# Narrow attentions of a one-core Trainium2 kernel: values and sums of two slices in one 32-column tile, six passes a batch for ten, merged by masked copies and a shuffle

## Chip, core and metric

The kernel runs on one core of one Trainium2 chip. The metric is the device time of one execution in microseconds (us), the median of the runs shown.

## What is computed

Four layers act on a residual `x` of 4 batches x 512 rows x 128 features. Each layer adds a cross-attention to 154 context rows and then a mixture of experts, each scaled by the tanh of a gate. Three of the four cross-attentions (layers 0, 2 and 3; the profile's names begin with L0x, L2x, L3x) have 16 heads of 8 features, and one function of the kernel makes all three:

```python
x = x + tanh(g_xattn[i]) * attention_i(layernorm(x), ctx)   # i = 0, 2, 3: 16 heads of 8
# attention: softmax(q k^T * scale) v, heads side by side, then @ Wo (+ bias)
x = x + tanh(g_ffn[i]) * experts_i(layernorm(x))
```

The softmax of a head needs two sums over the 154 keys: of weight times value (8 features) and of the weights alone. The kernel makes both on TensorE and divides afterwards.

## The kernel before, in words

`narrow_attention` (L800) writes out five instruction streams by hand (SyncE, GpSimd, TensorE, ScalarE, VectorE) that meet in counted semaphores. It loops over the 4 batches `b`; while the products of batch `b` are made, the scores of batch `f = b + 1` are made for their row maxima, and rows and queries of `g = b + 2` are prepared.

The 16 heads are 4 lanes (`j`, 32 partitions each) x 4 groups (`c`). The 154 keys are cut into 128 and a tail of 26, and the tails of all four groups share a fifth slice. So a batch has five slices (`SLOTS = 5`): c = 0..3 are the first 128 keys of one group, slice 4 (`NG`) is the tails.

On TensorE each batch goes through 12 score units `scores(f, i, i+1)` (L1134 to L1151), S0 to S11 here. All of them, for batches 1 to 3, write banks 0 and 1; so each waits until VectorE has taken the maxima of the one before (`maxima`, L1602, the reduction at L1611: `pe.wait_ge(s["mx"], n)`). Units have 3, 3 and 2 column blocks in turn: S2, S5, S8 and S11 are short. Between the units the stream places other work: `scoresT(b, c)` (L1161) makes the scores transposed, ScalarE's `exps` (L1398) makes weights of them in `pT` (two slices deep); `products(b, c)` (L1182, matmul L1198) multiplies by the values into bank 6 (`OUT`), and `sums(b, c)` (L1201, matmul L1210) multiplies the same weights by ones into bank 7 (`SUMS`). Each is a pass of four matmuls with 32 columns, one in each lane:

```python
nc.tensor.matmul(psum[32*j:32*j+32, OUT, :],  vz[:, b, x:x+32], pT[...], start=(c == 0), stop=(c == NG))   # products
nc.tensor.matmul(psum[32*j:32*j+32, SUMS, :], core.oz[:, c, :], pT[...], start=(c == 0), stop=(c == NG))   # sums
```

That is 5 + 5 passes a batch. `vz` holds each head's 8 value columns among zeros, in blocks 136 wide, so that the window of group c has its values in columns 8c to 8c + 7; `oz` has ones there. The order on TensorE within a batch is S0, row maxima, sums of the last tails, S1, scoresT 1, products 0, S2, queries, sums 0, S3, scoresT 2, S4, products 1, S5, sums 1, scoresT 3, S6, products 2, output of batch b - 1, S7, row maxima, sums 2, S8, scoresT 4, S9, products 3, S10, sums 3, S11, scoresT 0 and products of the tails (L1271 to L1330). The last batch (b = 3) has no score units; there `output(b-1, 1)` stands between the sums of slice 0 and scoresT 2.

After the tails ScalarE's `values` (L1406) copies both banks to SBUF (`ov`, `rsum`). VectorE's `normalised` (L1615) takes the reciprocal of 128 columns and multiplies, four times a batch, placed between the maxima of the next batch (after units 1, 2, 4 and 5); in the last batch it takes all 512 columns at once (L1746, L1759). TensorE's `output` (L1214) then multiplies each 128 columns by Wo as soon as they are there, `added` (L1628) adds the residual, `kept_in_parts` or `keep_rows` makes the next norm's statistics.

Ahead of the loop VectorE's `contexts` (L1541) fills `vz` and `vt` (values of the tails). `setup` (L82) makes constants on GpSimd; VectorE ends it with two copies (L181, L182).

Of the kernel before, what the change touches and what calls it, by code (L numbers as in the profile page):

```python
# [44 lines left out]
class Core:  # L45


    def __init__(self, nc, ctx):
# [33 lines left out]
def setup(core, io, loads, first):  # L82
# [3 lines left out]
    with ExitStack() as scope:  # L86
# [9 lines left out]
        with nc.Block() as block:  # L96
# [11 lines left out]
            def _(pool):  # L108
# [17 lines left out]
                nc.gpsimd.memset(core.oz[:], 0.0).then_inc(groups, 1)  # L126
# [5 lines left out]
                for c in range(4):  # L132
                    nc.gpsimd.memset(core.oz[:, c, 8 * c:8 * c + 8], 1.0)
# [5 lines left out]
                pool.wait_ge(groups, 7)  # L139
# [29 lines left out]
            def _(dve):  # L169
# [630 lines left out]
def narrow_attention(core, L, w, gate, kind, loaded, n_loads, late_loads=(), router=None, dispatch=None, pending=None):  # L800
# [21 lines left out]
    with ExitStack() as scope:  # L822
# [10 lines left out]
        vt = sb("vt", [P, B, NG, NG, DK])  # L833
# [4 lines left out]
        rsum = sb("rsum", [P, SEQ])  # L838
# [81 lines left out]
        with nc.Block() as block:  # L920
# [122 lines left out]
            def _(pe):  # L1043
# [138 lines left out]
                def products(b, c):  # L1182
                    n = SLOTS * b + c
                    if n < 0:
                        return
                    pe.wait_ge(s["pt"], NG * (n + 1))
                    if c == 0:
                        pe.wait_ge(s["vz"], b + 1)
                        pe.wait_ge(s["vt"], b + 1)
                        if b:  # L1190
                            pe.wait_ge(s["ov"], 2 * b - 1)
                        elif rope:
# [69 lines left out]
                if rope:  # L1262
                    pe.wait_ge(s["mx"], UNITS - 2)
                    keysT(1, SUMS)
                    queriesT(1, OUT)
                    pe.wait_ge(s["mx"], UNITS)
                if not rope:
                    pe.wait_ge(s["mx"], UNITS)
                    pe.wait_ge(s["bvb"], 1)
                    nc.tensor.matmul(psum[:, OUT, 0:D], bvb[:], w["wo"][:], start=True, stop=True).then_inc(s["bias_ps"], 1)  # L1270
                for b in range(B):  # L1271
# [24 lines left out]
                    sums(b, 0)  # L1296
# [12 lines left out]
                    sums(b, 1)  # L1309
# [8 lines left out]
                    sums(b, 2)  # L1318
# [10 lines left out]
                    sums(b, 3)  # L1329
# [12 lines left out]
            def _(act):  # L1342
# [2557 lines left out]
```

## Time and profile before

| | us |
|---|---|
| median of 3 runs | 1576.43 |
| lowest, highest run | 1574.64, 1577.44 |
| profiled execution, span from first to last instruction | 1592.2 |
| TensorE busy in it | 1297.0 |
| VectorE busy in it | 946.5 |
| ScalarE busy in it | 723.1 |

No time of the profiled execution beside its span is given; it was taken with the profiler on, and its span is 15.8 us (1.0%) above the median of the runs. Busy shares are averages over stages with different limits. In a row of the timeline the first two numbers are start and duration in us, and the bracket at the end gives the idle time of the engine before it and what ended that. An instruction that follows on the same engine can start a little before the duration of the one ahead is over.

### The profile page before, as it was taken

The numbers are of one execution on the slowest core, as the hardware profiler recorded it, in microseconds if no ns is written. First come the engines' busy times: TensorE is split into PE (matmuls) and PEld (weight loads), VectorE is DVE, ScalarE is ACT, GpSimd is POOL, SyncE is SP. The second block draws the span as 40 slices with busy tenths as digits, with TensorE's granted clock in tenths as the row PEclk, the third lists the DMA queues.
The fourth block names the chain that finished last, engine by engine and source line by source line (L and its number), as shares of the span: only waits on it lengthen the run. The fifth ranks groups of instructions, "written<-read, shape, count | busy, mean of one in ns | idle before, by whom it ended". The sixth has DMA issues, their size and how long they took to land. (4 is left out here: it accounts for less than half of the span.)

```text
span 1592.2 us, 25277 instructions
## 1 busy us (share of the span) xinstructions
PE 1297.0 (81%) x8946; PEld 752.5 (47%) x8946; DVE 946.5 (59%) x2139; ACT 723.1 (45%) x1940; POOL 527.5 (33%) x625
## 2 busy tenths in 40 slices
PE   2799629579989977784997698989887977996998
PEld 2444317345656645463442455656554434442443
DVE  6466621444555655255664688888764875555664
ACT  3354413166656533342543465655755333454222
POOL 2320340525333361333100365656643320000444
PEclk8599859799999997895998799999988996998999
DMA  2444120330000002322000000000000001000000
GB/s 65 127 130 128 40 66 26 72 75 14 1 1 2 1 27 62 89 58 50 9 10 2 1 1 1 1 2 1 1 1 1 1 10 23 10 3 1 7 7 14
DMA packets 66991, 45.30 MB, mean 28 GB/s; under 512 B 17564, under 2 KB 60261, under 8 KB 66869
## 3 DMA queue, kind: packets, MB, share of 16 engines
q1 hardware_dynamic: 61013, 34.48, 8.4%
q0 software_dynamic: 4096, 8.40, 1.9%
q8 instruction: 74, 1.21, 0.3%
q10 hardware_dynamic: 1760, 0.82, 0.3%
q14 instruction: 48, 0.39, 0.1%
HBM read 24.91 MB, written 13.89 MB: 24 GB/s over the span
## 5 line engine op out<-in xcount | busy, mean ns | idle before, releaser
L3411 ACT ACTIVATE L2a_pr<-psum,L2a_negmax 128x512 f32<-128x512 f32 (+3 forms) x256 | 132.6, 532 | 94.0 <-DVE L2a_negmax L3537 40.1
L557 ACT ACTIVATE L1x_praw<-psum,L1x_negmax 128x154 f32<-128x154 f32 x256 | 96.5, 392 | 78.4 <-DVE L1x_negmax L649 78.2
L318 POOL TENSOR_TENSOR L1x_pm<-L1x_praw,L1x_total 128x1024 f32<-128x1024 f32 x32 | 60.7, 1898 | 160.6 <-DVE L1x_total L655 111.7
L3276 PE MATMUL psum<-ident,L2a_pr 128*128 128x128 f32 x640 | 85.9, 278 | 19.0 <-DVE L2a_pT L3550 11.7
L649 DVE TENSOR_REDUCE L1x_negmax<-psum 128x4 f32<-128x616 f32 x64 | 50.7, 794 | 55.2 <-PE psum L370 51.0
L3276 PEld LDWEIGHTS psum<-ident,L2a_pr 128*128 128x128 f32 x640 | 71.7, 143 | 24.7 <-issue 21.1
L1978 POOL TENSOR_TENSOR L3f_scaled<-L3f_sg,L3f_wide 128x512 f32<-128x512 f32 (+1 forms) x44 | 55.7, 1271 | 66.9 <-ACT L3f_sg L2057 37.9
L1611 DVE TENSOR_REDUCE L3x_negmax<-psum 128x6 f32<-128x924 f32 (+1 forms) x48 | 47.7, 1011 | 46.8 <-PE psum L1149 37.4
L1611 DVE TENSOR_REDUCE L0x_negmax<-psum 128x6 f32<-128x924 f32 (+1 forms) x48 | 47.8, 1010 | 44.9 <-PE psum L1149 40.6
L3161 POOL TENSOR_TENSOR L2a_pr<-L2a_pr,L2a_total 128x1024 f32<-128x1024 f32 x29 | 56.5, 1947 | 46.5 <-DVE L2a_total L3566 46.3
L3164 POOL TENSOR_TENSOR L2a_pr<-L2a_pr,L2a_total 128x768 f32<-128x768 f32 x32 | 48.7, 1520 | 70.0 <-DVE L2a_total L3566 69.7
L1611 DVE TENSOR_REDUCE L2x_negmax<-psum 128x6 f32<-128x924 f32 (+1 forms) x48 | 47.8, 1011 | 32.6 <-PE psum L1149 27.8
L1404 ACT ACTIVATE L3x_pT<-psum 128x512 f32<-128x512 f32 x80 | 41.4, 606 | 50.3 <-PE psum L1175 41.8
L1404 ACT ACTIVATE L2x_pT<-psum 128x512 f32<-128x512 f32 x80 | 41.4, 605 | 49.0 <-PE psum L1175 40.5
L2057 ACT ACTIVATE L3f_sg<-psum 128x512 f32<-128x512 f32 (+1 forms) x44 | 26.3, 598 | 66.8 <-PE psum L2000 66.8
L3556 DVE COPY L2a_pT<-psum 128x768 f32<-128x768 f32 (+1 forms) x64 | 54.2, 846 | 3.3 <-PE psum L3276 3.3
L370 PE MATMUL psum<-L1x_kT,L1x_qT 64*128 64x154 f32 x512 | 52.6, 327 | 3.9 <-ACT L1x_qT L538 3.0
L1404 ACT ACTIVATE L0x_pT<-psum 128x512 f32<-128x512 f32 x80 | 41.4, 605 | 30.2 <-PE psum L1175 23.6
L3411 ACT ACTIVATION_READ_ACCUMULATOR L2a_pr<-psum,L2a_negmax 128x1 f32 x256 | 53.5, 209 | 0.0
L557 ACT ACTIVATION_READ_ACCUMULATOR L1x_praw<-psum,L1x_negmax 128x1 f32 x256 | 52.9, 207 | 0.0
L2878 PE MATMUL psum<-L1f_gu,L1f_xsT 128*128 x92 | 51.2, 645 | 1.1 <-ACT L1f_xsT L2931 1.1
L2000 PE MATMUL psum<-L3f_xnT,expert_arena 128*128 128x512 f32 (+1 forms) x88 | 46.7, 614 | 4.2 <-PEq L3822 4.2
(741 smaller groups left out, 3372.1 us busy)
## 6 DMA issues: line engine op xcount, KB each, us to landing
expert_arena<-in_L_ffn_w SPq DMA_DIRECT2D x16, 256.0 KB, 4.4
group_in<-zero SPq DMA_DIRECT2D x2, 1472.0 KB, 9.3
L1f_xs<-group_in SPq DMA_DIRECT2D x10, 256.0 KB, 3.8
group_out<-L1f_ys SPq DMA_DIRECT2D x10, 256.0 KB, 3.6
L1f_gu<-in_L_ffn_gate_up_w SPq DMA_DIRECT2D x8, 256.0 KB, 3.5
slots_in<-zero SPq DMA_DIRECT2D x1, 1280.0 KB, 9.0
L0f_xs<-slots_in SPq DMA_DIRECT2D x5, 256.0 KB, 3.6
resid<-in_x SPq DMA_DIRECT2D x4, 256.0 KB, 5.8
```

The lines of the kernel that those rows point to most:

```text
L318: nc.gpsimd.tensor_tensor(pm[:, n % 2].rearrange("p j t k -> p (j t) k"), praw[:, n % 3, :, :, 0:MAIN].rearrange("p j t k -> p (j t) k"), ...
L370: last = nc.tensor.matmul(psum[:, 2 * u + j, x * CTX:(x + 1) * CTX], qT[rows, g, t * P:(t + 1) * P], kT[rows, g, :], start=True, stop=True)
L557: nc.scalar.activation(praw[:, n % 3, j, t, :], psum[:, 2 * u + j, x * CTX:(x + 1) * CTX], ACT.Exp, bias=negmax[:, n % 2, u, j, x:x + 1], ...
L649: nc.vector.tensor_reduce(negmax[:, n % 2, u].rearrange("p j x -> p (j x)").rearrange("p (j x) -> p j x", x=2), psum[:, 2 * u:2 * u + 2, 0 ...
L1404: nc.scalar.activation(pT[:, (n % 2) * NG + j, :], psum[:, LANES + j, :], ACT.Exp, scale=scale).then_inc(s["pt"], 1)
L1611: nc.vector.tensor_reduce(negmax[:, f % 2, half, 2 * h:2 * h + 2, off:off + count], psum[:, bank:bank + 2, 0:count * CTX].rearrange("p j ( ...
L1978: nc.gpsimd.tensor_tensor(scaled[0:rows, n % 2, :], sg[0:rows, n % 3, :], wide[0:rows, picked_to(n) % SLANT, :], ALU.mult).then_inc(s["sca ...
L2878: nc.tensor.matmul(psum[:, UP[i % len(UP)], :], xsT[:, q % 2, t * P:(t + 1) * P], w["gu"][:, bass.ds(expert[i], 1), :].rearrange("p a f -> ...
L3161: ins = nc.gpsimd.tensor_tensor(x, x, inv[:, 0:2].unsqueeze(2).to_broadcast([P, 2, SEQ]), ALU.mult)
L3276: last = nc.tensor.transpose(psum[:, TURN + n // 4, n % 4 * P:(n % 4 + 1) * P], pr[:, m % RING, n * P:(n + 1) * P], core.ident[:])
L3411: ins = nc.scalar.activation(pr[:, i % RING, SEQ * j + lo:SEQ * j + hi], psum[:, bank + j, lo:hi], ACT.Exp, bias=negmax[:, i % RING, e:e + ...
L3556: nc.vector.tensor_copy(pT[:, q % 2, t:t + 7:3, heads, :], src[:, :, 0:3 * P].rearrange("p j (k x) -> p k j x", x=P))
```

## The change

The window of a group gets its ones beside its values: for groups 0 and 1 values go to rows 0 to 15 of a lane and sums to rows 16 to 31 of one bank (`EARLY`), for groups 2 and 3 sums go to rows 0 to 15 and values to rows 16 to 31 of the other (`LATE`). Four product passes and two tail passes make both. ScalarE splits the early bank by a mask per partition (`core.half`, columns 4 and 5) into `sm` and `ov`; VectorE adds the other half of the late bank to each, then swaps the halves of `sm` with a stream shuffle, so that sums stand on the rows of their values. The calls on VectorE move by one or two units.

```diff
-    LANES, OUT, SUMS = 2, 6, 7
+    LANES, EARLY, LATE = 2, 6, 7
+    SWAP = [(x + 16) % 32 for x in range(32)]
...
# TensorE: products and sums of five slices become products of four and two tails
-    nc.tensor.matmul(psum[32 * j:32 * j + 32, SUMS, :], core.oz[:, c, :] if c < NG else core.ot[:]..., ...)
+    pe.wait_ge(s["split"], 2 * b)       # before products 0, b > 0
+    pe.wait_ge(s["merged"], 2 * b)      # before products 2, b > 0
+    last = nc.tensor.matmul(psum[32 * j:32 * j + 32, EARLY if c < 2 else LATE, :], vz[:, b, x:x + 32], ..., start=(c % 2 == 0), stop=False)
+  def tail(b, late_half):
+    last = nc.tensor.matmul(psum[32 * j:32 * j + 32, LATE if late_half else EARLY, :], vt[b][:, j, 32 * late_half:32 * late_half + 32], ..., start=False, stop=True)
+    last.then_inc(s["pv" if late_half else "early"], 1)
...
-    products(b - 1, NG)
+    tail(b - 1, 0)
     scores(f, 0, 1)
     max_rows(2 * b + 1, lane(b, 0, 0))
-    sums(b - 1, NG)
+    tail(b - 1, 1)
...
-    sums(b, 0)
...
-    sums(b, 1)
...
-    sums(b, 2)
...
-    sums(b, 3)
...
# ScalarE
-    nc.scalar.activation(ov[:], psum[:, OUT, :], ACT.Copy).then_inc(s["ov"], 1)
-    nc.scalar.activation(rsum[:], psum[:, SUMS, :], ACT.Copy).then_inc(s["ov"], 1)
+    act.wait_ge(s["early"], b + 1)
+    nc.scalar.activation(sm[:], psum[:, EARLY, :], ACT.Identity, scale=core.half[:, 5:6]).then_inc(s["split"], 1)
+    nc.scalar.activation(ov[:], psum[:, EARLY, :], ACT.Identity, scale=core.half[:, 4:5]).then_inc(s["split"], 1)
...
+  def ones_in():     # five activations that write ones into vz and vt; called once, after filled(2)
...
# VectorE
-    nc.vector.tensor_tensor(vt[:, f], ...)
+    for half in range(2):
+        ins = nc.vector.tensor_tensor(vt[f][:, :, 48 * half:48 * half + 16]..., ...)
...
+  def merged(b, what):
+    if what == 0:
+        dve.wait_ge(s["pv"], SLOTS * (b + 1))
+    if what < 2:
+        dve.wait_ge(s["split"], 2 * b + 1 + what)
+        to, side = ((sm, 4), (ov, 5))[what]
+        nc.vector.scalar_tensor_tensor(out=to[:], in0=psum[:, LATE, :], scalar=core.half[:, side:side + 1], in1=to[:],
+                                       op0=ALU.mult, op1=ALU.add).then_inc(s["merged"], 1)
+    else:
+        dve.wait_ge(s["merged"], 2 * b + 1)
+        nc.vector.stream_shuffle(oT[:], sm[:], SWAP).then_inc(s["swapped"], 1)
...
     maxima(f, 1, 2)
-    normalised(b - 1, 0, 1)
+    merged(b - 1, 0)
     maxima(f, 2, 3)
-    normalised(b - 1, 1, 2)
+    merged(b - 1, 2)
     query_squares(g)
     maxima(f, 3, 4)
+    merged(b - 1, 1)
+    normalised(b - 1, 0, 1)
     maxima(f, 4, 5)
     query_inverted(g)
+    normalised(b - 1, 1, 2)
+    maxima(f, 5, 6)
     normalised(b - 1, 2, 3)
-    maxima(f, 5, 6)
+    maxima(f, 6, 7)
     normalised(b - 1, 3, 4)
-    maxima(f, 6, 7)
+    maxima(f, 7, 8)
     added(b - 1)
...
# last batch
+    for what in (0, 2, 1):
+        merged(b - 1, what)
     normalised(b - 1, 0, QT)
...
-    normalised(B - 1, 0, QT)
+    for what in (0, 2, 1):
+        merged(B - 1, what)
+    for t in range(QT):
+        normalised(B - 1, t, t + 1)
...
# setup: oz and its four memsets go; a mask `half` is made on GpSimd, and at the end of VectorE's stream
+    dve.wait_ge(groups, 9)
+    nc.vector.tensor_reduce(core.half[:, 4:5], core.half[:, 0:4], X_AXIS, ALU.add).then_inc(parts_made, 1)
+    dve.wait_ge(parts_made, NT + 2)
+    nc.vector.tensor_scalar(core.half[:, 5:6], core.half[:, 4:5], -1.0, 1.0, ALU.mult, ALU.add)
```

## Rows read from the trace of the kernel before

**Rows 1.** The page, parts 1 and 2: engines, and TensorE's granted clock in tenths.

```profile
PE 1297.0 (81%) x8946; PEld 752.5 (47%) x8946; DVE 946.5 (59%) x2139; ACT 723.1 (45%) x1940; POOL 527.5 (33%) x625
...
PEclk8599859799999997895998799999988996998999
```

**Rows 2.** Groups by line, layer 2's attention: count, busy us, mean ns, idle before.

```profile
L1210 PE MATMUL psum<-L2x_pT,oz 128*32 128x512 f32 x128 | 17.0, 604 | 0.0
```

**Rows 3.** Timeline of TensorE, layer 2, batch 1, units S2 to S7.

```profile
792.30 0.79 PE L1149 MATMUL psum<-L2x_k,L2x_q 32*128 32x154 f32 x8
...
794.08 1.07 PE L1210 MATMUL psum<-L2x_pT,oz 128*32 128x512 f32 x8
795.08 0.66 PE L1149 MATMUL psum<-L2x_k,L2x_q 32*128 32x154 f32 x6
...
797.35 1.05 PE L1149 MATMUL psum<-L2x_k,L2x_q 32*128 32x154 f32 x12 [0.36 <-DVE L2x_negmax L1611]
...
799.63 0.79 PE L1149 MATMUL psum<-L2x_k,L2x_q 32*128 32x154 f32 x8 [0.23 <-DVE L2x_negmax L1611]
...
802.31 0.95 PE L1149 MATMUL psum<-L2x_k,L2x_q 32*128 32x154 f32 x12
...
805.27 1.05 PE L1149 MATMUL psum<-L2x_k,L2x_q 32*128 32x154 f32 x12
...
806.79 1.06 PE L1210 MATMUL psum<-L2x_pT,oz 128*32 128x512 f32 x8
```

**Rows 4.** Timeline of VectorE in the same stretch.

```profile
798.45 1.12 DVE L1611 TENSOR_REDUCE L2x_negmax<-psum 128x6 f32<-128x924 f32 x1 [1.16 <-PE psum L1149]
799.49 0.94 DVE L1622 RECIPROCAL L2x_rsum<-L2x_rsum 128x128 f32<-128x128 f32 x1
800.47 0.29 DVE L1626 TENSOR_TENSOR L2x_oT<-L2x_ov,L2x_rsum 128x128 f32<-128x128 f32 x1
800.68 0.79 DVE L1611 TENSOR_REDUCE L2x_negmax<-psum 128x4 f32<-128x616 f32 x1
```

**Rows 5.** Groups by line, layer 2's attention: operations of VectorE and ScalarE on 128x512.

```profile
L1365 ACT ACTIVATE L2x_qc<-psum,L2x_bqc 128x512 f32<-128x512 f32 x2 | 1.4, 690 | 1.4 <-PE psum L1090 1.4
...
L770 DVE TENSOR_SCALAR resid<-L2x_oT 128x512 f32<-128x512 f32 x2 | 0.9, 427 | 0.1
...
L1509 DVE TENSOR_TENSOR L1f_gu<-L1f_dn 128x512 f32<-128x512 f32 x1 | 0.7, 679 | 0.0
```

**Rows 6.** Timeline of layer 2's last batch: VectorE and TensorE.

```profile
848.33 3.35 DVE L1622 RECIPROCAL L2x_rsum<-L2x_rsum 128x512 f32<-128x512 f32 x1 [3.72 <-ACT L2x_rsum L1413]
...
867.70 3.35 DVE L1622 RECIPROCAL L2x_rsum<-L2x_rsum 128x512 f32<-128x512 f32 x1 [11.76 <-ACT L2x_rsum L1413]
...
873.61 0.75 DVE L1634 SCALAR_TENSOR_TENSOR L2x_oT<-psum,gate,resid 128x512 f32<-128x512 f32 x1 [1.63 <-PE psum L1225]
...
852.16 1.13 PE L1225 MATMUL psum<-L2x_wo,L2x_oT 128*128 128x128 f32 x8 [2.09 <-DVE L2x_oT L1626]
```

**Rows 7.** Timeline of layer 3's last batch, TensorE: output of batch 2.

```profile
1437.87 1.13 PE L1225 MATMUL psum<-L3x_wo,L3x_oT 128*128 128x128 f32 x8 [2.25 <-DVE L3f_lg L1875]
```

**Rows 8.** Timeline at the end of layer 0's attention: GpSimd and VectorE.

```profile
191.07 0.96 POOL L2376 DMA_INDIRECT slots_in<-L0f_pair,L0f_to  x1 [0.30 <-issue]
191.31 0.17 DVE L774 TENSOR_SCALAR stat<-L0x_mv 128x8 f32<-128x8 f32 x1
```

**Rows 9.** Timeline ahead of the loops: VectorE in setup, ScalarE in layer 2.

```profile
12.49 0.47 DVE L182 TENSOR_SCALAR ctxp<-ctxT 128x616 f32<-128x616 f32 x1
...
747.85 0.59 ACT L1396 ACTIVATE L2x_mrow<-psum 8x512 f32<-8x512 f32 x1 [6.50 <-PE psum L1158]
```

**Rows 10.** Stretches: us, busy us (and count) of each engine, then the granted clock.

```profile
853.50:856.90 3.40, 3.40 (x20) 0.60 (x20) 2.33 (x11) 1.75 (x4) 0.00 (x0) 0.50 0.02 5
...
850.10:853.50 3.40, 1.34 (x12) 1.25 (x16) 2.66 (x6) 0.26 (x1) 0.00 (x0) 1.00 0.00 0
...
1433.80:1437.20 3.40, 1.82 (x16) 0.31 (x15) 3.37 (x4) 1.47 (x4) 0.00 (x0) 1.00 0.00 0
```

More of the change, by code:

```diff
@@ L125, in _ @@
                 nc.gpsimd.memset(core.quad[:], 1.0).then_inc(groups, 1)
-                nc.gpsimd.memset(core.oz[:], 0.0).then_inc(groups, 1)
+                nc.gpsimd.memset(core.half[:], 1.0).then_inc(groups, 1)
                 nc.gpsimd.memset(core.pen64[:], 0.0).then_inc(groups, 1)
@@ L138, in _ @@
                                         pattern=[[32, 4]], channel_multiplier=-1).then_inc(groups, 1)
-                pool.wait_ge(groups, 7)
+                nc.gpsimd.affine_select(out=core.half[:, 0:4], in_=core.half[:, 0:4], compare_op=ALU.is_ge, fill=0.0, base=0,
+                                        pattern=[[-32, 4]], channel_multiplier=1).then_inc(groups, 1)
+                pool.wait_ge(groups, 8)
+                nc.gpsimd.affine_select(out=core.half[:, 0:4], in_=core.half[:, 0:4], compare_op=ALU.is_ge, fill=0.0, base=15,
+                                        pattern=[[32, 4]], channel_multiplier=-1).then_inc(groups, 1)
                 nc.gpsimd.tensor_copy(core.ot[:], core.quad[:].unsqueeze(2).to_broadcast([P, 4, 8]))
@@ L832, in narrow_attention @@
         vz = sb("vz", [P, B, NG * WIDE])
-        vt = sb("vt", [P, B, NG, NG, DK])
+        vt_own = sb("vt", [P, B - 1, NG, 64])
+        vt = [vt_own[:, b] for b in range(B - 1)] + [core.x1[:, 14:16, :].rearrange("p n d -> p (n d)").rearrange("p (j e) -> p j e", j=NG)]
         negmax = sb("negmax", [P, 2, 2, NG, 2 * QT])
@@ L1180, in scoresT, with early_free @@
                                 last.then_inc(s["s2"], 1)
[L1182 to L1192, printed above, removed]
+                def early_free(b):
+                    pe.wait_ge(s["vz"], b + 1)
+                    pe.wait_ge(s["vt"], b + 1)
+                    if b:
+                        pe.wait_ge(s["split"], 2 * b)
+                    else:
+                        pe.wait_ge(s["ones_in"], 5)
+                        if rope:
                             pe.wait_ge(s["qc"], 2)
@@ L1333, in _ @@
                     dispatch.rowsT(pe, 1, 2, dispatch.rows, 1)
-                products(B - 1, NG)
-                sums(B - 1, NG)
+                tail(B - 1, 0)
+                tail(B - 1, 1)
                 if dispatch:
@@ L1450, in _ @@
                 filled(2)
+                ones_in()
                 if pending:
@@ L1561, in contexts @@
                     nc.vector.tensor_copy(heads[:, :, :, 0:DK], bank[:, 256:384].rearrange("p (c j d) -> p c j d", c=NG, j=NG)).then_inc(s["vz"], 1)
-                    nc.vector.tensor_tensor(vt[:, f], bank[:, 384:512].rearrange("p (c j d) -> p j c d", c=NG, j=NG),
-                                            core.quad[:].unsqueeze(1).unsqueeze(3).to_broadcast([P, NG, NG, DK]), ALU.mult).then_inc(s["vt"], 1)
+                    tails = bank[:, 384:512].rearrange("p (c j d) -> p j c d", c=NG, j=NG)
+                    for half in range(2):
+                        own = slice(2 * half, 2 * half + 2)
+                        ins = nc.vector.tensor_tensor(vt[f][:, :, 48 * half:48 * half + 16].rearrange("p j (c d) -> p j c d", c=2), tails[:, :, own, :],
+                                                      core.quad[:, own].unsqueeze(1).unsqueeze(3).to_broadcast([P, NG, 2, DK]), ALU.mult)
+                    ins.then_inc(s["vt"], 1)
                 def squares(x, rows, root):
```

90 lines of the change are left out of this document (54 added, 36 removed).

## The prediction, made before any run of the changed kernel

> **What bounds the kernel now.** I read the page first: TensorE is busy 81% of the span, VectorE 59%, ScalarE 45%, and the granted clock stands near full in the slices of the three narrow attentions (about 55 to 190, 755 to 875 and 1335 to 1460 us) [rows 1]. That says only that TensorE is the engine to watch. Then the groups by line of layer 2's attention: the sums have 128 records there, with 32 more for the tails, at 604 ns each [rows 2]. These overlap, so the price of a pass is read from the timeline: sums 0 starts at 794.08 and the next work at 795.08, 1.00 us [rows 3].
>
> Last the timelines of TensorE and VectorE side by side, unit by unit. Scores and maxima share one pair of banks, so units alternate. S4 starts at 797.35, its maxima at 798.45 take 1.12, S5 starts at 799.63 [rows 3, 4]: 2.28 us is the least for a long unit, however little stands in its gap. A short unit by the same steps: 0.79 scores, 0.05, 0.80 maxima, 0.06, so 1.70. TensorE's own scores take about 0.98 and 0.72 of this; a gap holds 1.30 or 0.98 of other work for nothing. Where it holds less, TensorE waits (0.36 and 0.23 before S4 and S5 [rows 3]). **So a removed pass is worth 1.00 only where its gap is overfull.**
>
> **What is removed.** Four passes a batch, 16 a layer, 48 in all: 48 us of TensorE at most. By gap:
> - Behind S2 (792.30 to 795.08, 2.78): queries and sums 0. Without the sums 1.78: 1.00 saved in batches 0 and 1. Batch 2 has no queries there, 0.72 + 1.00 = 1.72 against the least of 1.70: nothing.
> - Behind S5 (799.63 to 802.31, 2.68): sums 1 and scoresT 3. Without, 1.72: 0.96 saved in batch 0. In batches 1 and 2 a reciprocal and a multiplication stand ahead of the short maxima, which start 0.26 after the scores end instead of 0.05 [rows 3, 4]: 0.76.
> - Behind S7 (805.27 to 807.79, the latter being 806.79 + 1.00): row maxima and sums 2, 2.52. Without, the least of 2.28: 0.24. In layer 0, batches 0 and 1, a transposition of queries fills it further: 0.8.
> - Behind S10: sums 3 alone, 1.00 inside 1.30: nothing.
>
> **What is added and moved on VectorE.** The merge is a scalar_tensor_tensor of 128x512 from PSUM; L1634 is the same form, 0.75 [rows 6], 0.78 with its wait. Nothing in the trace is a shuffle. Its bounds are 0.43 (tensor_scalar, 128x512 in SBUF) and 3.35 (reciprocal, the slowest 128x512) [rows 5, 6]; I take 0.70, next to the tensor_tensor of that size, 0.68 [rows 5], which also moves one element in and out at a time. The Trainium skill (VectorE: DVE Perf Modes, The perf-mode tier table) gives a stream shuffle of 2,048 elements about 2.4 us, in the slowest tier; an estimate from it is 0.6 for 512, and the sum by it would be the same to within 1 us. No run here shows it yet.
>
> The first merge and the shuffle take the places of a reciprocal with its multiplication and are shorter: nothing. Two other places cost.
> - Between maxima 3 and 4 stand the second merge and the first reciprocal and multiplication. A reciprocal starts 1.04 after a reduction's start, the multiplication 0.98 after that, the next reduction 0.21 later [rows 4]: 1.04 + 0.78 + 0.98 + 0.21 = 3.01 from one long reduction to the next, where 2.28 is the least. S5 waits: 0.73 lost.
> - The fourth multiplication moves behind maxima 6, and the output of batch b - 1 behind S6 waits for it. S6 takes 0.95, 0.05 to its maxima, 1.04 + 0.98 + 0.29 to the product, about 0.3 for the last piece of output: 3.6 instead of 2.96 (802.31 to 805.27 [rows 3]). S7 and everything queued behind the output wait: 0.70 lost.
>
> Both hit batches 1 and 2. Products 2 now wait for both merges, with S7 and the output queued behind them on TensorE; the second merge follows maxima 3 and is over by then. Products 0 wait for both masked copies instead of one plain copy; these run in the same slots of ScalarE and end about as products 0 are due. `added`, a unit later, still ends as scoresT 4 needs its lane. Nothing for these three, and no DMA is moved: SyncE's queue keeps its order.
>
> **Sum of the loops.** Batch 0: 1.00 + 0.96 + 0.24 = 2.2 in layer 3; 1.85 in layer 2, where the pending rows of layer 1 fill VectorE behind maxima 2; 1.8 in layer 0, where squares of queries hold S4 and the first term falls away. Batch 1: 1.00 + 0.76 + 0.24 - 0.73 - 0.70 = 0.57 in layers 2 and 3, about 0 in layer 0. Batch 2: the same without the 1.00, a loss of 0.4, three times. Together 5.85 + 1.1 - 1.2 = **5.7 us saved**.
>
> **The last batch of each layer** has no score units. There the values of batch 2 are on the path: reciprocal at 848.33, output at 852.16 after 2.09 us of idle TensorE, then scoresT 2 [rows 6]; in layer 3 2.25 idle [rows 7]. Merge, shuffle, merge (0.78 + 0.72 + 0.78 = 2.3) replace two copies that ScalarE makes 0.5 apart; the masked copies themselves (Identity, 0.69 by L1365 [rows 5]) run under them. In layer 2 I get 849.6 instead of 848.33, 1.3 later; in the others 1.8. The sums that go shorten the way from scoresT 2 to the last slice again, by 1.3, 0.8 and 0.5 in layers 2, 3 and 0, since ScalarE's exponentials soon bind: 0, 1.0 and 1.3 late. TensorE then idles over 4 us, so some work there will run at half clock, as 853.5 to 856.9 does [rows 10]: 0.3, 0.5, 1.0. Behind the last tail: 1.0 for the merges, 0.4 for four reciprocals (4 x 1.18 against 3.35 + 0.9), less 0.7, as the output now runs under them: 0.7 each. Layer 0 ends with GpSimd at 192.03, VectorE at 191.48 [rows 8], so 0.5 of its delay is free. Ends: 2.5 + 1.0 + 2.2 = **5.7 us lost**.
>
> **Ahead of the loops.** Setup ends with VectorE's L182 [rows 9]; two small operations (0.17 each by L774 [rows 8]) and a wait follow it: 0.4. The second half of the tails' values delays layer 0's keys by 0.2. The five activations of ones are hidden in 6.50 us of idle ScalarE ahead of the row maxima [rows 9]; without that cover they would cost up to 5 x 0.69 a layer. GpSimd's setup loses and gains small operations: nothing.
>
> **Total:** 5.7 - 5.7 - 0.6, 0.6 us slower. The profiled span would be 1592.8 for 1592.2. The span stands 1.0% above the median of the runs; I carry the difference over: 1577.0.
>
> **Rivals.**
> - *VectorE hides its pieces.* If neither the 0.73 nor the 0.70 shows, six batches give 8.6 back: 1568.4. For it: VectorE is idle 1.16 ahead of a reduction [rows 4] and 41% of the span. Against it: both stand in its fixed order ahead of what TensorE waits for.
> - *TensorE's clock falls inside the loops*, slower. The loop now runs at 2.4 GHz; taken thinner, each of nine batches could lose one stretch as 853.5 to 856.9 to 1.2 GHz, 1.7 us each, 15 us: 1592. It decides from two such stretches in all (3.4 us). For it: the clock fell behind 2.09 idle us. Against: TensorE was busy 1.82 of 3.40 us around layer 3's 2.25 idle us and kept it, and the longest idle in a thinned loop is 1.3 [rows 7, 10]. The Trainium skill (TensorE: Matmul & The Clock Gate, Why this matters for your kernels) warns that idle gaps between bursts of matmuls put the engine back to half clock; by it, fewer passes can make the others dearer. The drop in rows 10 agrees, the kept clock shows that not every gap does it.
> - *The shuffle is dear.* At its upper bound 3.35 it adds 2.65 at six ends and, beyond 0.5 of slack, 2.2 in six batches: 29 us, 1606. It decides from about 1.1 us a shuffle. Only the range of unlike operations speaks for it.
>
> **Chances and range.** Forecast 0.55, its own range 1572 to 1582; hidden pieces 0.2; clock 0.1; shuffle 0.07; others, such as a wait I have overlooked, 0.08. A measurement of this kernel can tell about 0.2%, 3.2 us. The forecast case is mostly within it (0.45 of 0.55), with 0.06 above and 0.04 below; hidden pieces are faster but for 0.02; the clock and the shuffle slower but for 0.01; the rest is divided. Faster 0.24, same 0.49, slower 0.27. 1567 to 1586 leaves out most of the clock, the dear shuffle and the best of the hidden pieces.
>
> **What would show it.** Right: S2, S5 and S7 gaps of layer 2's batch 1 at 1.78, about 1.9 and 2.28; reduction 4 starting 0.7 late; TensorE waiting on the fourth multiplication ahead of S7; output of batch 2 in the last batch over 1 us later, and half clock behind it. Wrong: a loop batch shorter by 2 us or more, a shuffle far from 0.7 us, a granted clock of 0.5 between S0 and S11, or `ones_in` delaying the first row maxima.

## The result, and the profile after

The changed kernel takes 1610.62 us (median of 4 runs, 1603.22 to 1613.04) against 1576.93 for the kernel before beside it: a ratio of 1.021, 95% interval 1.019 to 1.023. It is 33.7 us slower; 1577.0 was forecast, with 1586 as the upper end. The profiled execution took 1608.59, its span is 1606.7. The mean granted clock of TensorE was 0.874 to 0.883 of full speed in the four runs, and 0.898 to 0.906 in ten runs of the kernel before (e6 below).

The page of the changed kernel, parts 1 and 2:

```profile
PE 1297.7 (81%) x8562; PEld 765.7 (48%) x8562; DVE 973.4 (61%) x2210; ACT 727.2 (45%) x1955; POOL 528.9 (33%) x623
...
PEclk8587758889999997896987799999998987897999
```

TensorE has 384 instructions fewer than in [rows 1] and is busy just as long: what it does takes longer. The clock line points at why. The third to fifth slice (80 to 200 us, most of layer 0's attention) stood at 9, 9, 8 and now stand at 8, 7, 7.

The first profile of before stood 16 us above its own runs, so the stages are compared with a second one, taken for e6 below (span 1572.4; the median of its runs is 1576.63). Stretches of batches 1 and 2 in layers 0, 2 and 3, each from the last row maxima of one batch to those of the next; columns are length, busy us (count) of TensorE, weight loads, VectorE, ScalarE and GpSimd, the granted clock, the share of the DMA engines and GB/s. The changed kernel:

```profile
95.36:135.33 39.97, 36.18 (x276) 20.86 (x274) 24.25 (x39) 17.13 (x31) 5.01 (x5) 0.69 0.46 118
135.33:170.44 35.11, 30.25 (x260) 15.34 (x256) 20.97 (x38) 14.13 (x26) 0.00 (x0) 0.79 0.39 101
782.55:812.72 30.17, 26.06 (x268) 13.55 (x270) 20.78 (x35) 13.93 (x27) 0.00 (x0) 1.00 0.07 12
812.72:846.40 33.68, 28.75 (x258) 15.24 (x256) 20.79 (x36) 12.32 (x24) 0.00 (x0) 0.81 0.01 2
1377.30:1409.19 31.89, 27.78 (x269) 13.66 (x270) 20.78 (x35) 14.26 (x27) 0.00 (x0) 0.96 0.06 11
1409.19:1438.47 29.28, 24.19 (x262) 12.67 (x264) 20.97 (x38) 14.14 (x27) 0.00 (x0) 1.00 0.01 2
sum 200.10, PE 173.20 PEld 91.33 DVE 128.54 ACT 85.91 POOL 5.01; mean PE 28.87 PEld 15.22 DVE 21.42 ACT 14.32 POOL 0.84
```

The kernel before (second profile), the same six stretches:

```profile
96.17:128.95 32.78, 30.61 (x312) 15.42 (x314) 22.42 (x36) 17.28 (x32) 5.05 (x5) 1.00 0.47 124
128.95:157.66 28.71, 27.67 (x294) 13.33 (x296) 19.16 (x34) 14.10 (x27) 0.00 (x0) 1.00 0.52 142
765.78:796.26 30.48, 29.37 (x300) 14.10 (x302) 19.00 (x32) 13.75 (x27) 0.00 (x0) 1.00 0.07 12
796.26:825.03 28.77, 27.66 (x294) 13.32 (x296) 18.99 (x31) 12.58 (x25) 0.00 (x0) 1.00 0.01 3
...
1379.44:1408.15 28.71, 27.66 (x294) 13.32 (x296) 19.16 (x34) 14.09 (x27) 0.00 (x0) 1.00 0.01 3
sum 179.93, PE 172.35 PEld 83.61 DVE 117.72 ACT 85.55 POOL 5.05; mean PE 28.72 PEld 13.93 DVE 19.62 ACT 14.26 POOL 0.84
```

Before, all six ran at 1.00. Now four of six have a lower clock, and the six together are 20.2 us longer. The two that kept 1.00 are near where the prediction put them: 30.17 for 30.48 (0.31 less; 0.57 was predicted) and 29.28 for 28.71 (0.57 more; 0.4 was predicted). Together these two are 0.3 us longer than before; the four at a lower clock carry 19.9 of the 20.2. The whole difference of the two spans, 34.3 us, by stages of the same two profiles:

| stage | before | after | difference |
|---|---|---|---|
| batches 1 and 2 of layers 0, 2, 3 | 179.9 | 200.1 | +20.2 |
| last row maxima to last transposed scores, three layers | 56.2 | 65.2 | +9.1 |
| from there to the end of the last output, three layers | 33.9 | 36.1 | +2.1 |
| first scores and batch 0, three layers | 155.2 | 152.3 | -2.9 |
| layer 2's last output to layer 3's first scores | 443.8 | 449.6 | +5.8 |
| all else | 703.4 | 703.3 | -0.1 |

**Where the clock falls.** TensorE in layer 2, from the output's wait in S6 to S9 or beyond, first batch 1, then batch 2, then a stretch of batch 2 with its granted clock (they answer to [rows 3]):

```profile
801.94 0.49 PE L1246 MATMUL psum<-L2x_wo,L2x_oT 128*128 128x128 f32 x2 [0.62 <-DVE L2x_oT L1678]
...
804.64 0.79 PE L1157 MATMUL psum<-L2x_k,L2x_q 32*128 32x154 f32 x8 [0.69 <-DVE L2x_negmax L1647]
...
806.46 1.05 PE L1157 MATMUL psum<-L2x_k,L2x_q 32*128 32x154 f32 x12
...
831.29 0.49 PE L1246 MATMUL psum<-L2x_wo,L2x_oT 128*128 128x128 f32 x2 [0.61 <-DVE L2x_oT L1678]
831.71 1.05 PE L1157 MATMUL psum<-L2x_k,L2x_q 32*128 32x154 f32 x12
...
833.98 1.40 PE L1157 MATMUL psum<-L2x_k,L2x_q 32*128 32x154 f32 x8 [0.69 <-DVE L2x_negmax L1647]
...
837.25 1.91 PE L1157 MATMUL psum<-L2x_k,L2x_q 32*128 32x154 f32 x12
...
844.16 0.63 PE L1157 MATMUL psum<-L2x_k,L2x_q 32*128 32x154 f32 x2 [1.29 <-DVE L2x_negmax L1647]
...
833.81:850.88 17.07, 15.61 (x108) 6.84 (x108) 6.19 (x16) 5.01 (x11) 0.00 (x0) 0.50 0.00 1
```

From S3 to the start of S8 the two batches are alike to 0.01 us: the output waits 0.6 for the fourth multiply, S8 waits 0.69 for the row maxima. Behind that, S9's scores take 1.91 instead of 1.05 in batch 2, where the granted clock is 0.5 (1.2 GHz) from 833.81 to 850.88, and batch 1 goes on at full clock. The longest idle time in either is 1.29 us; in batch 2 it comes only after the fall. In the kernel before S7 starts 2.96 behind S6; here it is 3.95, and S8 follows at 2.28.

Batch 1 has the work for its queries ahead of S3, which batch 2 has not. But batch 2 of layer 3 is like batch 2 of layer 2 to 0.01 us in every unit from S0 to S7, and it kept its clock:

```profile
1430.45 0.79 PE L1157 MATMUL psum<-L3x_k,L3x_q 32*128 32x154 f32 x8 [0.69 <-DVE L3x_negmax L1647]
...
1432.28 1.05 PE L1157 MATMUL psum<-L3x_k,L3x_q 32*128 32x154 f32 x12
```

The longest fall comes elsewhere. In layer 0's batch 1 the clock falls from 110.18 to 137.49, beginning in S4, ahead of the output's wait, behind an idle time of 1.65 us and within one of 0.83:

```profile
108.03 1.05 PE L1157 MATMUL psum<-L0x_k,L0x_q 32*128 32x154 f32 x12 [1.65 <-DVE L0x_negmax L1647]
...
110.91 0.62 PE L1157 MATMUL psum<-L0x_k,L0x_q 32*128 32x154 f32 x2 [0.83 <-DVE L0x_negmax L1647]
```

VectorE between the maxima of units 3 and 4 of batch 2, and ahead of the output (as [rows 4]):

```profile
821.81 1.12 DVE L1647 TENSOR_REDUCE L2x_negmax<-psum 128x6 f32<-128x924 f32 x1 [0.51 <-PE psum L1157]
822.85 0.74 DVE L1660 SCALAR_TENSOR_TENSOR L2x_ov<-psum,half,L2x_ov 128x512 f32<-128x512 f32 x1
823.50 0.94 DVE L1673 RECIPROCAL L2x_oT<-L2x_oT 128x128 f32<-128x128 f32 x1
824.48 0.29 DVE L1678 TENSOR_TENSOR L2x_oT<-L2x_ov,L2x_oT 128x128 f32<-128x128 f32 x1
824.69 1.11 DVE L1647 TENSOR_REDUCE L2x_negmax<-psum 128x6 f32<-128x924 f32 x1
...
830.94 0.29 DVE L1678 TENSOR_TENSOR L2x_oT<-L2x_ov,L2x_oT 128x128 f32<-128x128 f32 x1
```

One reduction follows the other by 2.88 (3.01 was predicted). The prices of the new operations, lines of the changed kernel by form (durations are least, median and greatest, in ns):

```profile
L1666 DVE STREAM_SHUFFLE L2x_oT<-L2x_sm x4: 716/721/731, 791.1 to 871.8; 128x512 f32<-128x512 f32 x4
...
L1660 DVE SCALAR_TENSOR_TENSOR L2x_ov<-psum,half,L2x_ov x4: 732/740/743, 793.5 to 872.4; 128x512 f32<-128x512 f32 x4
...
L1429 ACT ACTIVATE L2x_sm<-psum,half x4: 662/672/687, 787.2 to 870.1; 128x512 f32<-128x512 f32 x4
```

### The profile page after: what moved, and what is told of

It is laid out like the page before. It is cut to its first block and busy times, and to the rows that moved or that the text cites. A ratio compares the mean times of both kernels' runs of the same rounds, so it can differ in the third digit from the quotient of the medians.

```text
span 1606.7 us, 24645 instructions
## 1 busy us (share of the span) xinstructions
PE 1297.7 (81%) x8562; PEld 765.7 (48%) x8562; DVE 973.4 (61%) x2210; ACT 727.2 (45%) x1955; POOL 528.9 (33%) x623
## 5 line engine op out<-in xcount | busy, mean ns | idle before, releaser
L3471 ACT ACTIVATE L2a_pr<-psum,L2a_negmax 128x512 f32<-128x512 f32 (+3 forms) x256 | 132.0, 530 | 95.9 <-DVE L2a_negmax L3597 41.4
L563 ACT ACTIVATE L1x_praw<-psum,L1x_negmax 128x154 f32<-128x154 f32 x256 | 95.9, 390 | 79.2 <-DVE L1x_negmax L655 79.0
L3336 PE MATMUL psum<-ident,L2a_pr 128*128 128x128 f32 x640 | 85.7, 278 | 21.5 <-DVE L2a_pT L3610 12.9
L3336 PEld LDWEIGHTS psum<-ident,L2a_pr 128*128 128x128 f32 x640 | 71.7, 142 | 27.0 <-issue 23.3
L1647 DVE TENSOR_REDUCE L2x_negmax<-psum 128x6 f32<-128x924 f32 (+1 forms) x48 | 47.8, 1010 | 33.9 <-PE psum L1157 31.7
L1157 PE MATMUL psum<-L0x_k,L0x_q 32*128 32x154 f32 x384 | 45.5, 378 | 17.4 <-DVE L0x_negmax L1647 11.6
L1157 PEld LDWEIGHTS psum<-L0x_k,L0x_q 32*128 32x128 f32 x384 | 35.1, 237 | 46.2 <-DVE L0x_negmax L1647 30.2
```

Of the source, the lines that this page charges most:

```text
L563: nc.scalar.activation(praw[:, n % 3, j, t, :], psum[:, 2 * u + j, x * CTX:(x + 1) * CTX], ACT.Exp, bias=negmax[:, n % 2, u, j, x:x + 1], ...
L1157: last = nc.tensor.matmul(psum[:, bank + j % 2, k * CTX:(k + 1) * CTX], q4[rows, f % QB, c, t * P:(t + 1) * P], k4[rows, c, f, 0:CTX], sta ...
L1647: nc.vector.tensor_reduce(negmax[:, f % 2, half, 2 * h:2 * h + 2, off:off + count], psum[:, bank:bank + 2, 0:count * CTX].rearrange("p j ( ...
L3336: last = nc.tensor.transpose(psum[:, TURN + n // 4, n % 4 * P:(n % 4 + 1) * P], pr[:, m % RING, n * P:(n + 1) * P], core.ident[:])
L3471: ins = nc.scalar.activation(pr[:, i % RING, SEQ * j + lo:SEQ * j + hi], psum[:, bank + j, lo:hi], ACT.Exp, bias=negmax[:, i % RING, e:e + ...
```

## The experiments

The expectations speak of two theories. Theory 1: most of the loss is TensorE's clock, which falls to 1.2 GHz in the thinned loops. Theory 2: it is the merges and the waits they make, and the clock is a by-product. A dummy pass is four matmuls with zero weights that add nothing to the accumulators.

### e1: the four passes put back as dummies

```diff
+ def zeros(b, c): four matmuls, core.zero[:, 0:32] x pT of slice c, start=False, stop=False
  scores(f, 2, 3) ... + zeros(b, 0);  scores(f, 5, 6) + zeros(b, 1)
  scores(f, 7, 8) ... + zeros(b, 2);  scores(f, 10, 11) + zeros(b, 3)
```

> The changed kernel, with a dummy pass of four matmuls (zero weights onto the same accumulators) in each place where sums 0 to 3 stood: TensorE has the passes of the kernel before again, while VectorE and ScalarE keep the merges. Theory 1 (the 33.7 us come mostly from TensorE's clock, which falls to 1.2 GHz inside the thinned loops): no fall inside the loops, as in the kernel before; what stays is 0.6 us for each of 6 gaps S4, 1.0 us for each of 6 gaps S6, and 6 to 9 us in the three last batches: 1590 to 1596 us. Theory 2 (the added VectorE work and its waits cost it; the clock falls are incidental): 36 passes more in a kernel that is bound by its waits, with the half-clock stretches where they were: 1610 to 1628 us.

1602.6 us (ratio to before 1.017, 1.014 to 1.020): between the theories. The stretches of batch 1 of layer 0, and batches 2 of layers 2 and 3, then where the clock falls in the last of them, at S5:

```profile
95.87:131.67 35.80, 32.34 (x312) 16.00 (x314) 24.23 (x39) 17.46 (x32) 5.06 (x5) 0.95 0.43 110
805.77:836.02 30.25, 27.92 (x294) 13.39 (x296) 20.78 (x36) 12.64 (x25) 0.00 (x0) 1.00 0.01 2
1396.21:1430.35 34.14, 32.50 (x294) 15.65 (x296) 21.05 (x38) 14.15 (x27) 0.00 (x0) 0.85 0.01 2
...
1409.37 1.36 PE L1157 MATMUL psum<-L3x_k,L3x_q 32*128 32x154 f32 x8 [0.82 <-DVE L3x_negmax L1662]
```

Ten passes in place of six, and the six stretches are shorter: 194.5 us for 200.1. Where the clock stayed up, a batch is 1.5 longer than before the change (30.25 for 28.77), the two late gaps S4 and S6 at their price. But it still fell in two of six, so the dummies alone do not hold it. The fall in layer 3 begins at 1409.45, behind the wait for the maxima that the second merge delays (0.82) and ahead of this batch's output, so the wait of the output is not the only one that matters; in e5 the same wait of 0.82 us stays and the clock kept, so neither is it enough by itself.

### e2: one dummy pass, in S7

```diff
  scores(f, 7, 8); max_rows(2 * f, ...) + zeros(b, 2)
```

> The changed kernel with the dummy pass in one place alone, that of sums 2 in the gap after S7, which without it holds the row maxima alone. Theory 1a (the clock falls because of that one thin gap behind the wait of the output): the loops keep 2.4 GHz and the gap is 2.52 instead of 2.28 us: 1583 to 1592 us. Theory 1b (it falls because the whole loop is thinner): some falls stay, 1593 to 1608 us. Theory 2 (the waits cost it): 1610 to 1614 us.

1600.85 us (1.016, 1.014 to 1.018), theory 1b: with one pass more a batch the kernel takes 9.8 us less, and the clock still falls in the loops, for shorter stretches: the longest is 13.7 us for 27.3. In its profile the six stretches take 197.3 us for 200.1, so most of the 9.8 is not in them.

### e3: six passes without merges or waits

```diff
  sums(b, c):
+     if c < NG: return
- nc.scalar.activation(rsum[:], psum[:, SUMS, :], ACT.Copy)
+ nc.scalar.activation(rsum[:], core.oneb[:, 0:1].to_broadcast([P, SEQ]), ACT.Copy)
```

> The kernel before without the sums of the four full slices (TensorE has six passes a batch, as after the change) and with nothing in their place: VectorE and ScalarE keep their work and order, there is no merge; the denominators of the softmax are left out. By the gaps at 2.4 GHz this saves 1.0 us in each of 9 gaps S2, 0.8 in S5, 0.24 in S7, and some 2 to 4 us in the last batches: 1553 to 1557 us, which is what theory 2 expects (without the waits there is no loss). Theory 1 in the form that fewer passes alone let the clock fall: half-clock stretches inside the loops, 1565 to 1580 us. If the clock stays up here, it falls in the changed kernel by the thinner loop and the longer waits together.

1573.24 us (0.998, 0.997 to 1.000), where 1553 to 1557 was the price at full clock. Batches 1 and 2 of layer 2:

```profile
760.44:790.61 30.17, 27.29 (x268) 13.53 (x270) 19.01 (x32) 14.08 (x27) 0.00 (x0) 0.96 0.07 12
790.61:818.45 27.84, 23.89 (x258) 12.50 (x256) 18.98 (x32) 12.36 (x25) 0.00 (x0) 0.99 0.01 3
```

S0 to S11 of batch 1 came out at 26.03 us for 27.90, as the gaps promise, but the step to it from S11 of batch 0 took 4.16 for 2.58, at half clock, and gave most of that back. So even with nothing in return, removing the passes gains 2.4 us and not 20: fewer passes alone let the clock fall, though briefly (3.4 us at a time) in this profile. It is of a run of 1566.95 us, one of the two fastest of ten, whose mean granted clock was 0.896; in the ten it was 0.882 to 0.898. Nor are the 2.4 us all the passes' own: the profile has 524.4 us between layers 0 and 2 for 529.1, in code that the edit leaves alone but whose inputs it changes, and 421.4 in the three narrow layers for 425.3.

### e4: the output one gap later

```diff
  products(b, 2)
- if b and not ends: output(b - 1, lane(b, 3, 1))
  scores(f, 7, 8); max_rows(2 * f, lane(b, 3, 0))
+ if b and not ends: output(b - 1, lane(b, 3, 1))
```

> The changed kernel with the output projection of the batch before moved by one gap, from behind products 2 (gap S6) to behind the row maxima (gap S7): it no longer waits for the fourth multiply, and the thin gap S7 is filled. At 2.4 GHz S6 falls from 3.95 to 2.28 us and S7 rises from 2.28 to some 2.6, in 6 batches: 8 us less. Theory 2 (waits): 1601 to 1604 us, half-clock stretches where they were. Theory 1 (clock, set off by the wait in S6 and the thin S7 behind it): these stretches go from batches 1 and 2, 1577 to 1590 us.

1594.59 us (1.013, 1.009 to 1.017). S6 fell to 2.35 and S7 rose to 2.41. 16 us went, twice the 8 that the waits are worth at full clock, and the six stretches take 186.8 us for 200.1 in the profile. But it stays 4.6 above the range of theory 1: the clock still falls in each batch of layer 2, now behind the empty gap S10, and S11 takes 4.2 there for 2.58. Layer 2's batch 1:

```profile
775.34:805.95 30.61, 27.50 (x268) 13.68 (x262) 20.83 (x36) 13.95 (x27) 0.00 (x0) 0.95 0.07 12
```

### e5: both

```diff
  as e1, with zeros(b, 2) behind products(b, 2), and as e4
```

> The changed kernel with both at once: the four dummy passes (the one for sums 2 right behind products 2, in S6) and the output projection one gap later, in S7, so that no gap is thin and none waits for the fourth multiply. Theory 1 (the clock in the loops): 2.4 GHz throughout the loops, gaps S6 and S7 as in the kernel before (2.96 and 2.52 us), and what is left is 0.6 us for each of 6 gaps S4 and some 7 us in the three ends: 1584 to 1590 us. A rival in which layout or the work of VectorE costs beyond the gaps: above 1595 us.

1591.19 us (1.011, 1.010 to 1.013), 1.2 above the expected range. All six stretches are at full clock; layer 2's two and the sum of the six:

```profile
766.65:797.78 31.13, 29.40 (x300) 14.41 (x302) 20.86 (x36) 13.94 (x27) 0.00 (x0) 1.00 0.07 12
797.78:827.11 29.33, 27.62 (x294) 13.60 (x296) 20.85 (x35) 12.63 (x25) 0.00 (x0) 1.00 0.01 3
...
sum 182.49, PE 171.68 PEld 85.14 DVE 128.91 ACT 86.24 POOL 5.06; mean PE 28.61 PEld 14.19 DVE 21.48 ACT 14.37 POOL 0.84
```

VectorE does what it does in the changed kernel (128.91 us for 128.54), TensorE has the passes of before again, and 17.6 of the 20.2 us are gone. Of what stays, S4 is 3.6 (0.6 in each of six batches); the other gaps give 1.0 back. **With ten passes and the output moved, the merges cost the loops 2.6 us; the other 17.6 went with the clock and the wait in S6.** The profile is of one execution, the second fastest of six (1580.46 to 1596.71 us); the mean granted clock of the six is 0.896 to 0.909, about as in the kernel before. The profiled span is still 12.9 us longer than before: 11.1 of it in the ends (below), 6.1 between layers 2 and 3 (see e6) and 2.6 in the six stretches, less 5.9 in the first scores and batches 0 and 0.9 elsewhere.

### e6: the kernel before, again

```diff
  no change
```

> The kernel before, unchanged, for a second profile (the first was 16 us above its own runs): 1574 to 1578 us. Its three narrow layers, from the first score to the last output projection, should again take 424 us with 2.4 GHz from batch 1 on; if the stretches between them are 4 to 6 us shorter than in the changed kernel (529 and 450 us), that part of the loss lies outside the narrow loops.

1576.63 us. The narrow layers take 149.4, 135.8 and 140.1 us, 425 for the 424 expected. The first profile's surplus lay between layers 0 and 2, in layers the change leaves alone: 550.1 us there, 529.1 here. That stretch is as long in the changed kernel (529.0), but the one between layers 2 and 3 is not. By stretches as above, the changed kernel:

```profile
878.74:1328.36 449.62, 383.05 (x2517) 230.61 (x2517) 334.43 (x711) 242.12 (x724) 216.15 (x219) 0.92 0.01 2
```

The kernel before, second profile:

```profile
853.98:1297.79 443.81, 378.85 (x2517) 229.16 (x2517) 331.16 (x707) 242.16 (x724) 216.42 (x219) 0.93 0.01 2
```

The same 2517 matmuls are busy 4.2 us longer, and 74 us are at half clock for 65 before. The eight profiles with the merges have 447.3 to 450.0 us here, the two of the kernel before 443.8 and 443.9, and e3, e7, e8 and e9, without merges, 445.0 to 446.9. So a part of it comes with any change of what runs ahead, in code that is the same; what decides it was not tried, and these 5.8 us stay open.

### e7: only the sums of slices 0 and 1 removed

```diff
  sums(b, c):
+     if c < 2: return
```

> The kernel before without sums 0 and 1 alone (eight passes a batch; nothing is merged, and the denominators are replaced by a constant): the passes go from the two overfull gaps S2 and S5, and the gaps S7 and S10 keep theirs. At 2.4 GHz this saves 1.0 and 0.8 us in 9 batches, 16 us: 1557 to 1561 us if eight passes keep the clock up. If the clock falls as without all four: 1565 to 1578 us, and then no placing of fewer passes gains what the gaps promise.

1570.5 us (0.997, 0.995 to 0.999). Five of six stretches kept the clock, and layer 2's batches 1 and 2 are 28.81 and 28.07 for 30.48 and 28.77; the sixth, layer 0's batch 1, is 36.91 for 32.78. The 16 us were also too much: batch 2 has no queries in S2, so it saves 0.7, not 1.8. What the gaps promise comes in these batches, where the thin gaps keep their passes and the clock stays. The time of the whole kernel shows nothing of it: the three narrow layers together take 425.3 us, as before, and the profile is shorter by 5.0 between layers 0 and 2 (524.1 for 529.1), where only the inputs have changed.

### e8: the waits alone

```diff
  maxima(f, 5, 6)
- normalised(b - 1, 3, 4)
  maxima(f, 6, 7)
- added(b - 1)
+ normalised(b - 1, 3, 4)
  maxima(f, 7, 8)
- kept_in_parts(b - 1, 0)
+ added(b - 1)
  ... (one unit later each)
```

> The kernel before with all its ten passes, and only VectorE's order changed as the change has it: the fourth multiply behind row maxima 6, and addition and statistics one unit later. TensorE waits some 1.0 us more in S6 of 6 batches. If the wait costs what it lasts: 1581 to 1584 us, 2.4 GHz in the loops. If a wait of that length by itself lets the clock fall in a full loop: 1586 us or more, with half-clock stretches behind S6.

1580.8 us (1.002, 1.001 to 1.004), 4.3 more than before. S6 takes 3.85 instead of 2.96, and in a full loop the clock stays:

```profile
767.91:799.28 31.37, 29.64 (x300) 14.19 (x302) 18.91 (x32) 13.76 (x27) 0.00 (x0) 1.00 0.07 12
799.28:828.93 29.65, 27.92 (x294) 13.39 (x296) 18.90 (x31) 12.58 (x25) 0.00 (x0) 1.00 0.01 2
```

**So neither half alone makes the loss.** Passes gone: -2.4 us, with short falls of the clock. Wait added: +4.3, with none in the loops. Both, with the merges: +33.7. No run has six passes and the wait in S6 without the merges; e4, with six passes and the merges but without that wait, still has falls in the loops, where its six stretches are 6.9 us longer than before (3.6 of it S4), so the merges' own wait in S4 may have its part.

### e9, e11: the output of the last batch behind the next scores

```diff
- if ends: output(b - 1, 1)
  scores(f, 3, 4)
  scoresT(b, 2)
+ if ends: output(b - 1, 1)
```

> The kernel before, and in each layer's last batch the output projection of the third batch moved by one step of TensorE's order, behind the transposed scores of slice 2. In the profile TensorE idles 2.1 us there, until the third batch's multiplies are done, with these scores queued behind it. If the end of a layer hangs on that wait: 2.0 to 2.8 us less in each of three layers, 1568 to 1571 us. If the wait only moves: 1575 to 1578 us.

> The changed kernel with the same move in the last batches and nothing else. The stretch from the last row maxima to the last scores there is 2.6 to 3.3 us longer than before the change, by the merges (1.75 us until the reciprocal starts) and by half clock. If that chain is what the ends cost, hiding it behind the scores of slice 2 takes 3 us from each layer: 1599 to 1603 us, and the half-clock stretches in the loops stay. If the ends are long for another reason: 1608 to 1613 us.

In the kernel before it gains: 1574.04 us (0.998, 0.997 to 1.000), less than expected. Layer 2's output waits 0.62 instead of 2.09 us, with the scores ahead of it:

```profile
831.83 1.53 PE L1175 MATMUL psum<-L2x_q,L2x_k 32*128 32x512 f32 x8
833.98 1.13 PE L1225 MATMUL psum<-L2x_wo,L2x_oT 128*128 128x128 f32 x8 [0.62 <-DVE L2x_oT L1626]
```

The last row maxima to the last scores are 1.0, 2.7 and 1.1 us shorter in layers 0, 2 and 3. In the changed kernel the time fell by 7.4 to 1603.22 us (1.016, 1.012 to 1.020), 0.2 above the range of its first case, but not for its reason: the ends are only 0.4 and 1.1 shorter in layers 0 and 2 and 0.2 longer in layer 3, and about as long at half clock as they were (7 to 8 us each). The two profiles differ elsewhere, by 4.9 us less between the layers and 5.2 more in layer 3's batches 1 and 2. A miss: what of the 7.4 the move is worth is not shown.

The wait at that end in the changed kernel, TensorE in layer 2, answers to [rows 6]:

```profile
850.00 1.48 PE L1231 MATMUL psum<-L2x_pT,L2x_vt 128*32 128x512 f32 x8
...
857.44 1.81 PE L1246 MATMUL psum<-L2x_wo,L2x_oT 128*128 128x128 f32 x8 [3.90 <-DVE L2x_oT L1678]
```

### e10, e12: eight passes and no wait

```diff
  e10: as e4 and e11, and scores(f, 10, 11) + zeros(b, 3)
  e12: as e10, and in layer 0 zeros(b, 0) in S2, in each batch 0 zeros(b, 2) in S7
```

> The changed kernel with the output projection in S7 (as in e4), a dummy pass in the otherwise empty gap S10, where it costs nothing at 2.4 GHz, and the move in the last batches. At 2.4 GHz the loops are 11 us shorter than before the change (1.5, 0.7 and 1.5 us in batches 1, 2 and 0 of three layers), the merges at the end are hidden in part. If eight passes a batch and no wait in S6 keep the clock up: 1562 to 1570 us, below the kernel before. If the clock still falls in the loops: 1575 to 1592 us.

> As e10, with dummy passes in two more places where its profile shows TensorE waiting and the clock at 1.2 GHz: in layer 0 the one for sums 0 in S2 (there S3 ends with VectorE's query squares, so that the pass only shortens the wait behind it: S2 and S3 together 5.64 us without and 5.66 us with it in e1), and in each layer's batch 0 the one for sums 2 in S7, which has no output projection in that batch (2.28 us without, 2.51 with). Theory 1: work that is of no use makes it faster, by what e10 lost at half clock there, about 6 us in layer 0 and 5 us in layer 3, less 0.7: 1565 to 1570 us, below the kernel before. If the clock has nothing to do with TensorE's load: 1577 to 1581 us.

e10: 1576.88 us (1.000, 0.999 to 1.002), 33.7 less than the changed kernel by two moves and a pass that computes nothing. e12: 1572.59 us (0.9975, 0.9965 to 0.9985): below the kernel before, leaving nothing out, though short of 1565 to 1570. The stretch of e10 from layer 3's first scores to the end of batch 0, where the clock fell:

```profile
1298.74:1348.14 49.40, 41.86 (x392) 23.67 (x396) 27.93 (x34) 18.30 (x34) 5.06 (x4) 0.75 0.09 18
```

The same stretch of e12, 1302.49 to 1347.92, then its batches 1 and 2 of layer 2 and batch 1 of layer 0:

```profile
1302.49:1347.92 45.43, 38.11 (x400) 21.84 (x404) 27.94 (x34) 18.25 (x34) 5.08 (x4) 0.85 0.12 19
...
768.95:797.91 28.96, 26.85 (x276) 13.77 (x278) 20.83 (x36) 13.94 (x27) 0.00 (x0) 1.00 0.07 13
797.91:826.05 28.14, 24.98 (x270) 12.89 (x272) 20.84 (x36) 12.65 (x25) 0.00 (x0) 1.00 0.01 2
...
97.77:132.91 35.14, 30.90 (x296) 17.32 (x298) 24.33 (x40) 17.46 (x32) 5.05 (x5) 0.90 0.39 111
```

With one useless pass more, layer 3's stretch is 4.0 us shorter. In layer 0 the other pass did nothing of the kind: its batch 1 is 35.14 for e10's 34.80. That part of the expectation failed, and what layer 0 needs stays open. Against the kernel before beside each, e12 is 3.3 us faster and e9, which leaves the change out, 2.8, so the change itself has not been shown to pay. In the profiles e12 is shorter than e9 in the six stretches (177.3 us for 179.9) and in first scores and batches 0 (148.9 for 158.6), and loses that in the ends: 95.9 us from the last row maxima to the end of the output in three layers, for 85.3.

## Why the prediction was wrong

**The arithmetic at full clock held, but for S6.** S2, S5 and S7 of layer 2's batch 1 are 1.78, 1.90 and 2.28, as written. S4 lost 0.60 (0.73 predicted). The shuffle took 0.72 (0.70), the merge 0.74 (0.78), the masked copy 0.67 (0.69). The bounds around the shuffle were not needed; the estimate beside it from VectorE: DVE Perf Modes (the Trainium skill, The perf-mode tier table), 0.6, was near as well.

**S6 was mis-sized.** 3.6 was forecast, 3.95 measured, so 0.99 lost and not 0.70 (3.6 less 2.96 is in fact 0.65). The product ends at 831.23, the last two pieces of output start at 831.29 and S7 at 831.71, which is 0.48 where I gave 0.3. The maxima start 1.17 behind S6 (827.76 to 828.93), right behind the third multiplication on VectorE, where I gave 1.00.

**The step that failed: the sum of the loops prices every unit at full clock and has no term for a fall**, because the second rival, "TensorE's clock falls inside the loops", was given a chance of 0.1 and 1.7 us a batch. 5.7 us saved were forecast for the loops; batches 0 (with the first scores) became 2.9 shorter and batches 1 and 2 20.2 longer, 19.9 of it in four batches at a lower clock. The argument against it was that "the longest idle in a thinned loop is 1.3", shorter than the 2.25 us that the clock had survived in layer 3. For layer 2 the number was right (1.29 in the profile; 1.65 in layer 0), and it did not matter. In layer 2 the clock fell behind an idle time of 0.61 us in S6 and within one of 0.69 in S7, in layer 0 behind 1.65 and within 0.83, each shorter than the one that it survived before. Nor was what the prediction had itself found carried into this rival: that the output would wait in S6 just where S7 becomes the thinnest gap. And the price was too low, 1.7 us a batch: layer 0's batches 1 and 2 are 7.2 and 6.4 us longer, and a fall lasted up to 27 us (110.18 to 137.49). The point from which the rival said that it decides, 3.4 us in all, was passed by far.

The Trainium skill (TensorE: Matmul & The Clock Gate, Why this matters for your kernels), named beside that rival, points the right way: gaps put the engine back to half clock. Which gaps do it, the runs do not settle: with idle times of 0.61 and 0.69 us the clock fell in layer 2's batch 2 and stayed in layer 3's, and e8, whose longest idle time in layer 2's batch 2 is 0.62, had no fall.

**The ends**, a second term that was mis-sized, were put at 5.7 us and cost 11.2 (9.1 and 2.1 in the table). Behind the last tails the 2.1 is what the prediction has (3 x 0.7). In the last batch 4.1 was forecast (2.3 of delay, 1.8 of half clock), 9.1 was measured. One part is that layer 2's loop already handed it a half clock: its tails take 1.48 and 1.94 us instead of 1.06, the output starts 3.5 later, and its wait of 3.90 us lowers the clock once more. In e5, with the loops at full clock, the ends of the three layers are still 3.0, 2.4 and 3.4 us longer, so most of the loss there is the end's own: merges, then half clock.

**Ahead of the loops** 0.6 was forecast. First scores and batch 0 are 2.9 us shorter where 5.85 less 0.6 was due; layer 3's batch 0 ran at half clock from 1366.29 to its end, and layer 2's first two units in batch 0 took 4.07 and 5.41 us at half clock, for 3.10 and 2.84 before.

**Carrying the first profile's surplus of 15.8 us over** was right, as e6 shows: they lay in layers that the change leaves alone. The nearest number of all that were written down, 1606, belongs to the third rival, the dear shuffle, and would have been luck: the shuffle took 0.72 us. The second rival named the cause, with 1592.

## What to carry to other kernels

Where a tuned loop keeps TensorE at its full clock only by being full, taking a pass out may not save its duration, and may cost more than it saves: look at the granted clock with each edit, and put the thin gaps and the waits of a loop in different places. Take work out of gaps that are overfull and leave the gaps that have room their work; a dummy pass in an empty one is a cheap test, and in e2 and in layer 3 of e12 it was worth more than it cost. Price the same instruction from rows at 0.5 and at 1.0, and ask at which of the two the changed loop will run, before its gaps are added up.

## What the runs showed of the hardware that was not expected

- The clock fell in layer 2, where no idle time in batches 1 and 2 is above 1.29 us. Of two batches alike to 0.01 us up to the start of S8 (batch 2 of layers 2 and 3) one fell to 1.2 GHz and one kept 2.4. So where the fall comes is not set by the batch alone; what else sets it was not found.
- Once down, it stayed down for 13.7 to 27.3 us in the four longest falls of the changed kernel's loops; ahead of the one in layer 2 it had been at full clock for 71.7 us. At half clock the same scores take 1.91 instead of 1.05 us.
- Passes with zero weights held the clock as the real sums had where the output was moved too (e5, one profile); with the output in its place it fell in two of six stretches (e1).
- Passes removed and a wait added cost -2.4 and +4.3 us apart and, with the merges, +33.7 together: the prices do not add. What the merges' own wait has in this was not run by itself.
